# A decoder layer on one core: the score matmuls of query and key in scaled fp16 halves instead of fp32r and fp32

## The chip, the cores and the metric

The kernel runs on one core of one Trainium2 chip, in one launch. The metric is the device time of the launch in microseconds (us). The core has TensorE (PE; its weight loads are shown apart as PEld), VectorE (DVE), ScalarE (ACT), GpSimd (POOL) and SyncE (SP), which here only issues transfers. Engines run their own instruction streams and meet at semaphores.

## The reference

A decoder layer for 8 batches of 256 tokens, 512 wide. The change is in its first part, a linear attention with decay over 16 heads of 128:

```python
qkv = jax.nn.silu(x @ Wqkv.T).reshape(b, n, h, 3 * d)      # b, n, h, d = 8, 256, 16, 128
q, k, v = jnp.split(qkv, 3, axis=-1)
# in blocks of 64 with a carried state; written out, for i >= j:
#   out[i] = sum_j  exp(-s * (i - j)) * (q[i] . k[j]) * v[j]
rms = jax.lax.rsqrt(jnp.mean(out * out, axis=-1, keepdims=True) + eps)
gate = jax.nn.sigmoid(x @ Wg.T)
x = layernorm(x + (gate * (out * rms * norm_w)) @ Wo.T)
x = layernorm(x + wkv(time_decay, time_first, x, ctx))     # a recurrence over the 256 tokens
x = layernorm(x + bitlinear(gelu(bitlinear(x, w_fc)), w_proj))   # ternary weights, 512 -> 2048 -> 512
```

All inputs and the output are fp32.

## The kernel before

The attention is worked head by head: 8 *pairs* of heads, 8 *units* in a pair. Unit t of a pair is head t % 2 on token group t // 2, 512 tokens, which are two batches of 256. There are 64 units. A unit projects Q, K and G (the gate) with three fp16 matmuls for each of 4 slices of the 512 inputs (`project`; x and the weights are split in fp16 halves `x_hi`, `x_lo`, `w_hi`, `w_lo`, scaled so that they fit, and the product hi*lo + lo*hi + hi*hi is taken), ScalarE evacuates Q and K through Silu to fp32 tiles `q_t` and `k_t` with the product of the inverse scales, `dq`, as its scale, and V is projected for both heads at once (`project_v`). The halves of a head's weights are made by VectorE (`split_w`), the halves of x by ScalarE and VectorE (`split_x`), both from bounds that TensorE spreads over the partitions (`w_bound`, `x_bound`, with a matmul by ones).

For each of a unit's two batches `scores` makes keys by queries. Since a query sees only earlier keys, keys 0 to 127 meet all 256 queries (256 columns), keys 128 to 255 only the last 128 (128 columns). The wide part takes three fp32r matmuls of halves (`q_hi`, `q_lo`, `k_hi`, `k_lo`, where the k halves are made for the first keys only), the narrow part one fp32 matmul of `k_t` and `q_t`, which the trace shows as two records. VectorE multiplies both parts by the decays into `probs` (`mask`), splits them (`split_probs`), and `mix` multiplies by V. VectorE then gates the result (`gate`: `gated`, `u_hi`, `u_lo`), and `output` multiplies by Wo; VectorE adds the four token tiles of each unit to `resid` (`add_y`).

The order of every engine is written out by hand. TensorE's for unit u is: scores of unit u - 1, projection of Q, two tiles of output of unit u - 2, projection of K, two more tiles, mix of unit u - 1, projection of G, projection of V. VectorE's for unit u:

```python
                    mask(u - 1, 1 - i, 0)
                    mask(u - 1, 1 - i, 1)
                    split_v(u - 1, (t - 1) % PER_PAIR)
...
                    split_probs(u - 1)
                split_q(u)
...
                split_k(u)
...
                if not (t == 7 or last_pair and t == 7):
                    dequant(p, t + 1)
```

with the adds between these, and behind `dequant` (which makes `dq` for the next unit) the splits of weights (t = 0, 7), a chunk of the feed-forward weights (after_unit) and the gate. Pair 0 also splits x for the other groups; the last pair also starts the recurrence of the second part (`input_sum`, `bb_states`, `aa_states`, `correct`, and on GpSimd `weighted`, `numerator` and others), so that the third part can follow at once. Between pair 2 and pair 3 all engines pass through the mean of the feed-forward weights (`abs_two`).

Of the kernel before, what the change touches and what calls it, by code (L numbers as in the profile page):

```python
# [41 lines left out]
def decoder_layer(nc, x_t, x_rows, ctx_t, w_heads, slopes, norm_w, decay, first, w_ffn, out):  # L42
# [6 lines left out]
    with ExitStack() as ctx:  # L49
# [45 lines left out]
        dqv = sb("dqv", [P, GROUPS])  # L95
        stats = sb("stats", [P, 4, BT, 6])
# [40 lines left out]
        q_hi = sb("q_hi", [P, GT], F32R, att)  # L137
        q_lo = sb("q_lo", [P, GT], F32R, att)
        k_hi = sb("k_hi", [P, 2, P], F32R, att)
        k_lo = sb("k_lo", [P, 2, P], F32R, att)  # L140
# [62 lines left out]
        wmax_ok, wbound_ok, winv_ok = sem("wmax_ok"), sem("wbound_ok"), sem("winv_ok")  # L203
        wscale_ok, whalf_ok, dq_ok = sem("wscale_ok"), sem("whalf_ok"), sem("dq_ok")
# [178 lines left out]
        def _(pe):  # L383
# [48 lines left out]
            def scores(u, b):  # L432

                pe.wait_ge(q_split, u + 1)
                pe.wait_ge(k_split, u + 1)
                wait(pe, masked, 2 * u + b - 1)
                o = b * SEQ
                wide = SC[b][:, 0:SEQ]
                mm(wide, k_hi[:, b, :], q_hi[:, o:o + SEQ], start=True, stop=False)
                mm(wide, k_hi[:, b, :], q_lo[:, o:o + SEQ], start=False, stop=False)  # L440
                mm(wide, k_lo[:, b, :], q_hi[:, o:o + SEQ], start=False, stop=True)
                mm(SC[b][:, SEQ:SEQ + P], k_t[:, o + P:o + SEQ], q_t[:, o + P:o + SEQ],  # L442
                   start=True, stop=True).then_inc(scored, 1)
# [267 lines left out]
        def _(act):  # L711
# [100 lines left out]
            def unit(p, t, first_pair=False, last_pair=False):  # L812
# [5 lines left out]
                split_q(u)  # L818
# [6 lines left out]
                split_k(u)  # L825
# [162 lines left out]
        def _(dve):  # L988
# [59 lines left out]

            def dequant_v(g):
# [713 lines left out]
```

## Time and profile before

| | |
|---|---|
| time, median of 3 runs | 1334.83 us (1333.92 to 1334.94) |
| profiled execution, its own time | 1334.65 us |
| its span | 1332.9 us |
| granted TensorE clock, mean | 0.995 |
| attention (pairs 0 to 7) | from the start to about 1050 us |
| TensorE, VectorE, ScalarE, GpSimd busy | 97%, 73%, 47%, 22% |

The profile is one execution. Its own time and its span differ by 1.75 us around the first and last instruction. Busy time counts the length of instructions; a matmul's record is longer than the time after which the next one can start, since they overlap, so what a matmul costs is read from the distance of starts in the timeline and not from its length.

### The profile page before, as it was taken

To read this page: it belongs to the slowest core of one execution; us is meant where nothing else is said; L and a number is where in the kernel's file an instruction comes from. 1 tells how busy PE (TensorE), PEld (TensorE's weight loads), DVE (VectorE), ACT (ScalarE), POOL (GpSimd) and SP (SyncE) were. 2 spreads that over 40 slices of the span, in tenths; PEclk is the share of its full clock that TensorE was granted. 3 is DMA by queue.
4 is the path that set the end of the run, shared out by engine and by line. 5 is a ranking of instruction groups with operands and counts; after the bars stand their busy time and mean duration, and the time that the engine had idled before them with its cause. 6 is when DMAs were issued, how large, how long until landed. Compare 5 with 4: busy or idle time off the path is not lost.

```text
span 1332.9 us, 20153 instructions
## 1 busy us (share of the span) xinstructions
PE 1289.5 (97%) x7468; PEld 830.8 (62%) x7468; DVE 967.8 (73%) x1882; ACT 629.6 (47%) x1138; POOL 298.2 (22%) x213
## 2 busy tenths in 40 slices
PE   5899999999999999999999999999998999999997
PEld 3566666666666666666666666666665555555553
DVE  6875776696577667766776677667678788998763
ACT  3443343344333433533353344334356678888854
POOL 2112111111110111111111111111125565555630
PEclk9999999999999999999999999999999999999999
DMA  5100021121111111011111110001010111110000
GB/s 186 60 17 16 25 88 32 48 80 64 33 65 32 48 32 41 24 49 32 40 53 36 32 49 32 32 16 41 1 48 17 33 32 48 48 48 32 17 17 32
DMA packets 19103, 55.83 MB, mean 42 GB/s; under 512 B 2624, under 2 KB 2624, under 8 KB 18624
## 3 DMA queue, kind: packets, MB, share of 16 engines
q1 hardware_dynamic: 19008, 54.55, 12.3%
q8 instruction: 61, 1.00, 0.3%
q14 instruction: 34, 0.28, 0.1%
HBM read 50.35 MB, written 4.19 MB: 41 GB/s over the span
## 4 chain that ended last, share of the span: by engine, by line
PE 59%; DVE 5%; ACT 3%; issue 2%; POOL 1%; ACTq 0%; POOLq 0%; DVEq 0%
PE bank L399 7%; PE bank L400 7%; PE bank L401 7%; PE bank L613 4%; PE bank L614 4%; PE bank L471 3%; PE bank L473 3%; PE bank L472 3%; PE bank L414 3%; PE bank L416 2%; PE bank L415 2%; PE bank L639 2%; PE bank L638 2%; PE bank L459 1%; PE bank L442 1%
## 5 line engine op out<-in xcount | busy, mean ns | idle before, releaser
L399 PE MATMUL bank<-x_hi,w_hi 128*128 128x512 f16 x768 | 294.6, 384 | 5.2 <-DVE w_lo L1076 2.9
L1122 DVE TENSOR_TENSOR resid<-resid,bank 128x512 f32<-128x512 f32 x256 | 173.2, 686 | 173.5 <-PE bank L473 172.9
L400 PE MATMUL bank<-x_lo,w_hi 128*128 128x512 f16 x768 | 293.8, 383 | 0.0
L401 PE MATMUL bank<-x_hi,w_lo 128*128 128x512 f16 x768 | 293.2, 382 | 0.0
L1578 POOL TENSOR_TENSOR sq_sum<-sq_sum,o_sq 128x512 f32<-128x512 f32 x64 | 106.6, 1665 | 797.0 <-ACT o_sq L757 797.0
L757 ACT ACTIVATE o_sq<-bank 128x512 f32<-128x512 f32 x64 | 38.3, 599 | 287.9 <-DVE gated L1128 287.9
L414 PE MATMUL bank<-wv_hi,x_hi 128*128 128x256 f16 x512 | 139.6, 273 | 1.0 <-DVE x_lo L1137 0.6
L416 PE MATMUL bank<-wv_hi,x_lo 128*128 128x256 f16 x512 | 139.6, 273 | 0.0
L415 PE MATMUL bank<-wv_lo,x_hi 128*128 128x256 f16 x512 | 139.6, 273 | 0.0
L399 PEld LDWEIGHTS bank<-x_hi,w_hi 128*128 128x128 f16 x768 | 76.5, 100 | 91.9 <-issue 19.9
L401 PEld LDWEIGHTS bank<-x_hi,w_lo 128*128 128x128 f16 x768 | 75.7, 99 | 92.5 <-issue 3.3
L471 PE MATMUL bank<-wo_hi,u_hi 128*128 128x512 f32 x256 | 122.8, 480 | 3.2 <-DVE resid L1122 2.8
L400 PEld LDWEIGHTS bank<-x_lo,w_hi 128*128 128x128 f16 x768 | 75.7, 99 | 70.6 <-issue 2.2
L1094 DVE TENSOR_TENSOR probs<-bank,decays 128x256 f32<-128x256 f32 x128 | 53.9, 421 | 88.8 <-PE bank L442 52.9
L744 ACT ACTIVATE q_t<-bank,dq 128x512 f32<-128x512 f32 x64 | 44.1, 689 | 125.6 <-PE bank L401 125.4
L744 ACT ACTIVATE k_t<-bank,dq 128x512 f32<-128x512 f32 x64 | 44.0, 688 | 121.4 <-PE bank L401 121.4
L473 PE MATMUL bank<-wo_hi,u_lo 128*128 128x512 f32 x256 | 101.2, 395 | 0.0
L613 PE MATMUL bank<-tern,xq_hi 128*128 128x512 f16 x256 | 97.1, 379 | 3.0 <-ACT hid L883 3.0
L472 PE MATMUL bank<-wo_lo,u_hi 128*128 128x512 f32 x256 | 99.7, 390 | 0.0
L614 PE MATMUL bank<-tern,xq_lo 128*128 128x512 f16 x256 | 97.0, 379 | 0.0
L638 PE MATMUL bank<-tern,hq_hi 128*128 128x512 f16 x256 | 97.0, 379 | 0.0
L639 PE MATMUL bank<-tern,hq_lo 128*128 128x512 f16 x256 | 97.0, 379 | 0.0
(174 smaller groups left out, 2660.2 us busy)
## 6 DMA issues: line engine op xcount, KB each, us to landing
w_raw<-w_ffn SPq DMA_DIRECT2D x32, 512.0 KB, 3.5
raw_a<-w_heads SPq DMA_DIRECT2D x32, 256.0 KB, 3.8
raw<-w_heads SPq DMA_DIRECT2D x15, 512.0 KB, 3.6
raw<-w_heads SPq DMA_DIRECT2D x18, 256.0 KB, 3.9
x_in<-x_rows SPq DMA_DIRECT2D x8, 512.0 KB, 3.8
out<-y_out SPq DMA_DIRECT2D x8, 512.0 KB, 2.6
resid<-x_t SPq DMA_DIRECT2D x3, 1024.0 KB, 8.0
val<-ctx_t SPq DMA_DIRECT2D x6, 512.0 KB, 3.5
```

Of the source, the lines that this page charges most:

```text
L399: mm(bk[:, :], a, c, start=kt == 0, stop=False)
L400: mm(bk[:, :], a, d, start=False, stop=False)
L401: last = mm(bk[:, :], b, c, start=False, stop=kt == KT - 1)
L414: mm(to[:, o:o + 2 * DH], a, e, start=kt == 0, stop=False)
L415: mm(to[:, o:o + 2 * DH], a, f, start=False, stop=False)
L416: last = mm(to[:, o:o + 2 * DH], b, e, start=False, stop=kt == KT - 1)
L471: mm(YB[tt % 2][:, :], u_hi[:, c], wo_hi[:, i, :], start=True, stop=False)
L472: mm(YB[tt % 2][:, :], u_hi[:, c], wo_lo[:, i, :], start=False, stop=False)
L473: mm(YB[tt % 2][:, :], u_lo[:, c], wo_hi[:, i, :], start=False, stop=True).then_inc(y_done, 1)
L613: mm(FC[f % 2][:, :], xq_hi[:, t, kt, :], w, start=kt == 0, stop=False)
L614: last = mm(FC[f % 2][:, :], xq_lo[:, t, kt, :], w, start=False, stop=kt == KT - 1)
L1122: tt(resid[:, 4 * g + t, :], resid[:, 4 * g + t, :], YB[t % 2][:, :], ALU.add).then_inc(y_added, 1)
```

## The change

The four tiles of halves become fp16 and cover all 512 keys and queries. Before they are rounded, q and k are multiplied by a scale each, `qk_scale`, which VectorE works out for each unit from `dq` (`score_scales`: three small instructions in a chain, behind each `dequant`); the product of the inverse scales, `s_dq`, goes into the masks, which become scalar_tensor_tensor instructions with that scalar read from memory. ScalarE's rounding of q and k takes the scale, and VectorE's low halves too. Both parts of the scores now take three fp16 matmuls. A spare tile keeps the other tiles where they were. Its core:

```diff
-        q_hi = sb("q_hi", [P, GT], F32R, att)
-        q_lo = sb("q_lo", [P, GT], F32R, att)
-        k_hi = sb("k_hi", [P, 2, P], F32R, att)
-        k_lo = sb("k_lo", [P, 2, P], F32R, att)
+        q_hi = sb("q_hi", [P, GT], F16, att)
+        q_lo = sb("q_lo", [P, GT], F16, att)
+        k_hi = sb("k_hi", [P, GT], F16, att)
+        k_lo = sb("k_lo", [P, GT], F16, att)
+        sb("spare1", [P, GT], F32, att)
...
-                wide = SC[b][:, 0:SEQ]
-                mm(wide, k_hi[:, b, :], q_hi[:, o:o + SEQ], start=True, stop=False)
-                mm(wide, k_hi[:, b, :], q_lo[:, o:o + SEQ], start=False, stop=False)
-                mm(wide, k_lo[:, b, :], q_hi[:, o:o + SEQ], start=False, stop=True)
-                mm(SC[b][:, SEQ:SEQ + P], k_t[:, o + P:o + SEQ], q_t[:, o + P:o + SEQ],
-                   start=True, stop=True).then_inc(scored, 1)
+                for out, k0, q0, q1 in ((SC[b][:, 0:SEQ], o, o, o + SEQ), (SC[b][:, SEQ:SEQ + P], o + P, o + P, o + SEQ)):
+                    kh, kl = k_hi[:, k0:k0 + P], k_lo[:, k0:k0 + P]
+                    mm(out, kh, q_hi[:, q0:q1], start=True, stop=False)
+                    mm(out, kh, q_lo[:, q0:q1], start=False, stop=False)
+                    last = mm(out, kl, q_hi[:, q0:q1], start=False, stop=True)
+                last.then_inc(scored, 1)
...
-            def split_q(u):
+            def split_q(u, t):
                 act.wait_ge(evacuated, PROJ * u + Q + 1)
-                fn(q_hi[:, :], q_t[:, :], ACT.Copy).then_inc(q_hi_ok, 1)
-
-            def split_k(u):
+                act.wait_ge(qk_scale_ok, u + 1)
+                fn(q_hi[:, :], q_t[:, :], ACT.Identity, scale=qk_scale[:, t % 2, t // 2, 0:1]).then_inc(q_hi_ok, 1)
+
+            def split_k(u, t):
                 act.wait_ge(evacuated, PROJ * u + K + 1)
-                fn(k_hi[:, :, :], first_keys(k_t), ACT.Copy).then_inc(k_hi_ok, 1)
+                fn(k_hi[:, :], k_t[:, :], ACT.Identity, scale=qk_scale[:, t % 2, t // 2, 1:2]).then_inc(k_hi_ok, 1)
...
+            def score_scales(p, t):
+
+                u, g, i = PER_PAIR * p + t, t // 2, t % 2
+                dve.wait_ge(dq_ok, u + 2)
+                ts(qk_inv[:, i, g, :], dq[:, i, g, 0:2], 131072.0, TINY, ALU.mult, ALU.add).then_inc(qk_inv_ok, 1)
+                dve.wait_ge(qk_inv_ok, u + 1)
+                v.reciprocal(qk_scale[:, i, g, :], qk_inv[:, i, g, :]).then_inc(qk_scale_ok, 1)
+                ts(s_dq[:, i, g:g + 1], qk_inv[:, i, g, 0:1], qk_inv[:, i, g, 1:2], None, ALU.mult).then_inc(s_dq_ok, 1)
...
-                tt(probs[:, b, 0:SEQ], SC[b][:, 0:SEQ], decays[:, i, :], ALU.mult).then_inc(masked_off, 1)
-                tt(probs[:, b, SEQ:SEQ + P], SC[b][:, SEQ:SEQ + P], decays[:, i, 0:P], ALU.mult).then_inc(masked, 1)
-
-            def split_q(u):
+                stt(probs[:, b, 0:SEQ], SC[b][:, 0:SEQ], c, decays[:, i, :], ALU.mult, ALU.mult).then_inc(masked_off, 1)
+                stt(probs[:, b, SEQ:SEQ + P], SC[b][:, SEQ:SEQ + P], c, decays[:, i, 0:P], ALU.mult,
+                    ALU.mult).then_inc(masked, 1)
+
+            def split_q(u, t):
                 dve.wait_ge(q_hi_ok, u + 1)
                 wait(dve, scored, 2 * u)
-                tt(q_lo[:, :], q_t[:, :], q_hi[:, :].bitcast(F32), ALU.subtract).then_inc(q_split, 1)
-
-            def split_k(u):
+                stt(q_lo[:, :], q_t[:, :], qk_scale[:, t % 2, t // 2, 0:1], q_hi[:, :], ALU.mult,
+                    ALU.subtract).then_inc(q_split, 1)
+
+            def split_k(u, t):
                 dve.wait_ge(k_hi_ok, u + 1)
-                tt(k_lo[:, :, :], first_keys(k_t), k_hi[:, :, :].bitcast(F32), ALU.subtract).then_inc(k_split, 1)
+                stt(k_lo[:, :], k_t[:, :], qk_scale[:, t % 2, t // 2, 1:2], k_hi[:, :], ALU.mult,
+                    ALU.subtract).then_inc(k_split, 1)
...
                 if not (t == 7 or last_pair and t == 7):
                     dequant(p, t + 1)
+                    score_scales(p, t + 1)
...
                     dequant(p + 1, 0)
+                    score_scales(p + 1, 0)
...
             dequant(0, 0, K, V)
+            score_scales(0, 0)
             split_w(0, 0, K, 2)
```

TensorE, the scores of unit 0, between the projection of V (`wv_hi`, `x_lo`) and the next projection of Q (`x_hi`, `w_hi`), before:

```order
L416 MATMUL bank<-wv_hi,x_lo 128x256
L430 MATMUL bank<-wmax,ones 128x3
L439 MATMUL bank<-q_hi,k_hi 128x256
L440 MATMUL bank<-q_lo,k_hi 128x256
L441 MATMUL bank<-q_hi,k_lo 128x256
L442 MATMUL bank<-q_t,k_t 128x128
L439 MATMUL bank<-q_hi,k_hi 128x256
L440 MATMUL bank<-q_lo,k_hi 128x256
L441 MATMUL bank<-q_hi,k_lo 128x256
L442 MATMUL bank<-q_t,k_t 128x128
L399 MATMUL bank<-x_hi,w_hi 128x512
```

and now (the first batch, and the start of the second, which is the same):

```order
L421 MATMUL bank<-wv_hi,x_lo 128x256
L435 MATMUL bank<-wmax,ones 128x3
L445 MATMUL bank<-q_hi,k_hi 128x256
L446 MATMUL bank<-q_lo,k_hi 128x256
L447 MATMUL bank<-q_hi,k_lo 128x256
L445 MATMUL bank<-q_hi,k_hi 128x128
L446 MATMUL bank<-q_lo,k_hi 128x128
L447 MATMUL bank<-q_hi,k_lo 128x128
L445 MATMUL bank<-q_hi,k_hi 128x256
```

In place of one fp32 matmul of 128 columns stand three fp16 ones; nothing else of TensorE has moved.

VectorE in unit 0, from the low halves of q and k to the split of unit 1's weights (`w_hi`, `w_lo`), before:

```order
L1100 TENSOR_TENSOR q_lo<-q_t,q_hi 128x512
L1104 TENSOR_TENSOR k_lo<-k_t,k_hi 128x256
L1013 TENSOR_REDUCE wmax<-raw 128x3
L1025 TENSOR_SCALAR winv<-bank 128x3
L1027 RECIPROCAL wscale<-winv 128x3
L1030 TENSOR_SCALAR winv<-winv 128x1
L1047 TENSOR_SCALAR dq<-winv,xinv 128x3
L1073 TENSOR_SCALAR w_hi<-raw,wscale 128x512
L1076 SCALAR_TENSOR_TENSOR w_lo<-raw,wscale,w_hi 128x512
```

and now:

```order
L1118 SCALAR_TENSOR_TENSOR q_lo<-q_t,qk_scale,q_hi 128x512
L1123 SCALAR_TENSOR_TENSOR k_lo<-k_t,qk_scale,k_hi 128x512
L1019 TENSOR_REDUCE wmax<-raw 128x3
L1031 TENSOR_SCALAR winv<-bank 128x3
L1033 RECIPROCAL wscale<-winv 128x3
L1036 TENSOR_SCALAR winv<-winv 128x1
L1053 TENSOR_SCALAR dq<-winv,xinv 128x3
L1059 TENSOR_SCALAR qk_inv<-dq 128x2
L1061 RECIPROCAL qk_scale<-qk_inv 128x2
L1062 TENSOR_SCALAR s_dq<-qk_inv 128x1
L1088 TENSOR_SCALAR w_hi<-raw,wscale 128x512
L1091 SCALAR_TENSOR_TENSOR w_lo<-raw,wscale,w_hi 128x512
```

The three scale instructions stand between `dq` and the weights' split, and k_lo is twice as wide.

## Rows read from the trace of the kernel before

**Rows 1.** The page's busy time, share and instructions of each engine.

```profile
PE 1289.5 (97%) x7468; PEld 830.8 (62%) x7468; DVE 967.8 (73%) x1882; ACT 629.6 (47%) x1138; POOL 298.2 (22%) x213
```

**Rows 2.** Windows: stretch, length, busy us of each engine, clock, DMA share, GB/s.

```profile
145.00:270.00 125.00, 125.00 (x750) 84.49 (x748) 88.32 (x177) 47.82 (x86) 14.51 (x10) 1.00 0.16 51
...
905.00:1060.00 155.00, 145.30 (x844) 96.27 (x843) 120.80 (x230) 79.79 (x139) 51.32 (x35) 1.00 0.08 25
```

**Rows 3.** Timeline of TensorE: start us, length us, line, tiles, shape, how many.

```profile
601.13 0.27 PE L414 MATMUL bank<-wv_hi,x_hi 128*128 128x256 f16 x1
...
603.65 0.27 PE L416 MATMUL bank<-wv_hi,x_lo 128*128 128x256 f16 x1
...
603.88 0.28 PE L440 MATMUL bank<-q_lo,k_hi 128*128 128x256 f32 x1
...
604.12 0.38 PE L442 MATMUL bank<-q_t,k_t 128*128 128x128 f32 x2
...
604.70 0.38 PE L442 MATMUL bank<-q_t,k_t 128*128 128x128 f32 x2
604.91 0.38 PE L399 MATMUL bank<-x_hi,w_hi 128*128 128x512 f16 x1
...
607.29 0.38 PE L401 MATMUL bank<-x_hi,w_lo 128*128 128x512 f16 x1
```

**Rows 4.** Groups of weight loads by shape: count, busy us, mean ns.

```profile
L414 PEld LDWEIGHTS bank<-wv_hi,x_hi 128*128 128x128 f16 x512 | 50.0, 98 | 14.8 <-issue 2.4 <-DVE wv_lo L1065 0.4
...
L442 PEld LDWEIGHTS bank<-q_t,k_t 128*128 128x128 f32 x256 | 39.4, 189 | 0.0
```

**Rows 5.** Groups of VectorE by shape.

```profile
L1402 DVE SCALAR_TENSOR_TENSOR hq_lo<-bank,h_scale,hq_hi 128x512 f16<-128x512 f32 x64 | 46.8, 743 | 33.8 <-ACT hq_hi L927 33.8
L1100 DVE TENSOR_TENSOR q_lo<-q_t,q_hi 128x512 fp32r<-128x512 f32 x64 | 44.9, 701 | 0.0
L1128 DVE SCALAR_TENSOR_TENSOR gated<-g_t,bank 128x512 f32<-128x512 f32 x64 | 43.5, 679 | 1.5 <-PE bank L459 1.5
...
L1104 DVE TENSOR_TENSOR k_lo<-k_t,k_hi 128x256 fp32r<-128x256 f32 x64 | 28.0, 437 | 2.2 <-ACT k_hi L765 2.2
```

**Rows 6.** Timeline of VectorE, small instructions ahead of unit 1's weight split.

```profile
31.93 0.15 DVE L1030 TENSOR_SCALAR winv<-winv 128x1 f32<-128x1 f32 x1
32.12 0.23 DVE L1047 TENSOR_SCALAR dq<-winv,xinv 128x3 f32<-128x3 f32 x1
32.26 0.48 DVE L1073 TENSOR_SCALAR w_hi<-raw,wscale 128x512 f16<-128x512 f32 x1
```

**Rows 7.** Groups of ScalarE by shape.

```profile
L765 ACT ACTIVATE k_hi<-k_t 128x256 fp32r<-128x256 f32 x64 | 26.7, 418 | 2.0
...
L723 ACT ACTIVATE x_hi<-resid,xscale 128x512 f16<-128x512 f32 x16 | 10.2, 711 | 11.4 <-DVE xscale L1005 11.4
```

**Rows 8.** Timeline of TensorE, its waits: [us idle before <-who ended it].

```profile
18.82 0.60 PE L399 MATMUL bank<-x_hi,w_hi 128*128 128x512 f16 x1 [2.08 <-DVE w_lo L1076]
...
33.58 0.39 PE L399 MATMUL bank<-x_hi,w_hi 128*128 128x512 f16 x1 [0.82 <-DVE w_lo L1076]
...
39.29 0.50 PE L423 MATMUL bank<-xmax,ones 128*128 128x4 f32 x2 [2.94 <-DVE probs L1095]
...
66.28 0.27 PE L414 MATMUL bank<-wv_hi,x_hi 128*128 128x256 f16 x1 [0.28 <-DVE x_lo L1137]
...
398.71 0.38 PE L689 MATMUL bank<-abs_two,ones 128*128 128x2 f32 x2 [2.08 <-DVE abs_two L1276]
...
995.47 0.27 PE L414 MATMUL bank<-wv_hi,x_hi 128*128 128x256 f16 x1 [0.43 <-DVE rms_in L1498]
...
1019.29 1.09 PE L587 MATMUL bank<-ident,num 128*128 128x128 f32 x8 [1.46 <-DVE probs L1095]
...
1041.05 0.50 PE L471 MATMUL bank<-wo_hi,u_hi 128*128 128x512 f32 x1 [2.83 <-DVE resid L1122]
```

**Rows 9.** Timeline of VectorE in the last pair.

```profile
996.49 2.82 DVE L1133 TENSOR_TENSOR u_lo<-gated,u_hi 128x512 fp32r<-128x512 f32 x1
```

More of the change, by code:

```diff
@@ L95, in decoder_layer @@
         dqv = sb("dqv", [P, GROUPS])
+        qk_inv = sb("qk_inv", [P, 2, GROUPS, 2])
+        qk_scale = sb("qk_scale", [P, 2, GROUPS, 2])
+        s_dq = sb("s_dq", [P, 2, GROUPS])
         stats = sb("stats", [P, 4, BT, 6])
@@ L203, in decoder_layer @@
         wmax_ok, wbound_ok, winv_ok = sem("wmax_ok"), sem("wbound_ok"), sem("winv_ok")
+        qk_inv_ok, qk_scale_ok, s_dq_ok = sem("qk_inv_ok"), sem("qk_scale_ok"), sem("s_dq_ok")
         wscale_ok, whalf_ok, dq_ok = sem("wscale_ok"), sem("whalf_ok"), sem("dq_ok")
@@ L817, in unit @@
                 evacuate(u, t, Q, first_unit)
-                split_q(u)
+                split_q(u, t)
                 if lag1:
@@ L824, in unit @@
                 evacuate(u, t, K, first_unit)
-                split_k(u)
+                split_k(u, t)
                 if last_pair and t in (4, 5):
@@ L1088, in split_wo, with mask @@
                 tt(wo_lo[:, i, :], raw_a[:, i, :], wo_hi[:, i, :].bitcast(F32), ALU.subtract).then_inc(wo_split, 1)
-            def mask(u, i, b):
+            def mask(u, t, b):
+                i, c = t % 2, s_dq[:, t % 2, t // 2:t // 2 + 1]
                 dve.wait_ge(scored, 2 * u + b + 1)
+                dve.wait_ge(s_dq_ok, u + 1)
                 wait(dve, mixed, u)
-                tt(probs[:, b, 0:SEQ], SC[b][:, 0:SEQ], decays[:, i, :], ALU.mult).then_inc(masked_off, 1)
-                tt(probs[:, b, SEQ:SEQ + P], SC[b][:, SEQ:SEQ + P], decays[:, i, 0:P], ALU.mult).then_inc(masked, 1)
-            def split_q(u):
+                stt(probs[:, b, 0:SEQ], SC[b][:, 0:SEQ], c, decays[:, i, :], ALU.mult, ALU.mult).then_inc(masked_off, 1)
+                stt(probs[:, b, SEQ:SEQ + P], SC[b][:, SEQ:SEQ + P], c, decays[:, i, 0:P], ALU.mult,
+                    ALU.mult).then_inc(masked, 1)
+            def split_q(u, t):
                 dve.wait_ge(q_hi_ok, u + 1)
                 wait(dve, scored, 2 * u)
-                tt(q_lo[:, :], q_t[:, :], q_hi[:, :].bitcast(F32), ALU.subtract).then_inc(q_split, 1)
-            def split_k(u):
+                stt(q_lo[:, :], q_t[:, :], qk_scale[:, t % 2, t // 2, 0:1], q_hi[:, :], ALU.mult,
+                    ALU.subtract).then_inc(q_split, 1)
+            def split_k(u, t):
                 dve.wait_ge(k_hi_ok, u + 1)
-                tt(k_lo[:, :, :], first_keys(k_t), k_hi[:, :, :].bitcast(F32), ALU.subtract).then_inc(k_split, 1)
+                stt(k_lo[:, :], k_t[:, :], qk_scale[:, t % 2, t // 2, 1:2], k_hi[:, :], ALU.mult,
+                    ALU.subtract).then_inc(k_split, 1)
             def split_v(u, t):
@@ L1148, in unit @@
                         dve.wait_ge(decays_ok, 2 * p + t)
-                    mask(u - 1, 1 - i, 0)
-                    mask(u - 1, 1 - i, 1)
+                    mask(u - 1, (t - 1) % PER_PAIR, 0)
+                    mask(u - 1, (t - 1) % PER_PAIR, 1)
                     split_v(u - 1, (t - 1) % PER_PAIR)
@@ L1158, in unit @@
                     split_probs(u - 1)
-                split_q(u)
+                split_q(u, t)
                 if t == 0 and not first_pair:
@@ L1178, in unit @@
                     add_y(u - 2, gb, 3)
-                split_k(u)
+                split_k(u, t)
                 if first_pair and t in (1, 2, 4):
@@ L1510, in _ @@
             U = UNITS
-            mask(U - 1, 1, 0)
-            mask(U - 1, 1, 1)
+            mask(U - 1, PER_PAIR - 1, 0)
+            mask(U - 1, PER_PAIR - 1, 1)
             split_v(U - 1, PER_PAIR - 1)
```

## The prediction

> **What bounds the kernel now.** I read the busy line first: TensorE is busy 97% of the span, VectorE 73% [rows 1]. The windows then say where TensorE is not full. From 145 to 270 us it is busy for the whole stretch, with VectorE at 71% (88.32 of 125.00), while from 905 to 1060 us it lacks 9.7 us and VectorE is busy for 120.80 of 155.00 [rows 2]. So in the middle of the attention (pairs 1 to 6) the end moves by what a unit costs on TensorE, and VectorE's extra work is free there; at the start, at the step before pair 3 and in the last pair TensorE waits for VectorE, and there VectorE's extra work counts. The list of TensorE's waits names these places [rows 8].
>
> **TensorE, removed and added.** The two score blocks of one unit stand in the timeline [rows 3]. The 24 fp16 matmuls of 256 columns of the V projection start from 601.13 to 603.65, 0.110 us apart, so the first score matmul's turn comes at 603.76, and the next projection starts at 604.91: 1.15 us for both blocks. Inside, an fp32r matmul of 256 columns takes 0.12 (from the second at 603.88 to the fourth instruction at 604.12 is 0.24), three of them 0.36; the second block's fp32 one of 128 columns, which shows as two records, takes 0.21 (604.70 to 604.91). 2 x (0.36 + 0.215) = 1.15.
>
> After, each block has three fp16 matmuls of 256 columns and three of 128. The first three have V's shape, 0.1096 each: 0.66 for six. fp16 with 128 columns is not in the trace. From below, 128 columns can't take less than their share of the pace of wider ones: the 12 of 512 columns of a projection start from 604.91 to 607.29, 0.216 apart, 256 take 0.110, so the slope is 0.415 ns a column and 128 come to 0.056. From above, each matmul has a weight load of its own, whose record in fp16 is 98 ns long [rows 4]; if nothing of it overlapped with a matmul as short as this, the pace would be 0.098. I take 0.058, near the lower end, because loads overlap in the rows: an fp32 load's record is 189 ns long and yet its matmuls follow each other at 0.11 to 0.12, some 0.07 less, and the same 0.07 off 98 ns leaves 0.03, well below 0.056. A unit then costs 0.658 + 6 x 0.058 = 1.006 and saves 0.144 us; with 0.056 it saves 0.154, with 0.098 it loses 0.096.
>
> The Trainium skill (TensorE: Matmul & The Clock Gate, section "Back-to-back issue gap") speaks against the change. It gives about 81 ns per matmul at 128 columns for streams of loads and matmuls in real kernels, and an isolated gap of N/2.4 + 2.5 ns, which is 56 ns. By 81 ns a unit would save 0.01 us. The same sentence gives 131 ns at 512 columns, where this trace shows 215, and the isolated form gives 216; so I hold to the second.
>
> 64 units have scores. About 60 keep the saving; in the others TensorE comes to a wait on VectorE that has no TensorE work ahead of it in its chain (33.58, 39.29 and some in the last pair). 60 x 0.144 = **8.6 us gained**.
>
> **VectorE and ScalarE, added in each unit.** A scalar read from memory costs a scalar_tensor_tensor 0.063 us: 743 ns with one against 679 without, same columns, both with a PSUM operand [rows 5]. The masks are now such instructions, four a unit: +0.25. q_lo goes from 701 to about 750: +0.05. k_lo has all 512 columns: from 437 to about 750, +0.31. The three small scale instructions stand in a chain; in the rows a dependent small one starts 0.19 after the one it waits for, 0.04 after its end, and an instruction that waits for nothing new 0.14 after dq, whose scalar is in memory and which lasts 0.23 [rows 6]. dq's successor used to start 0.14 behind it; now it stands behind qk_inv (0.23 + 0.04 after dq), the reciprocal (0.19 on), s_dq (estimated half of that, 0.09, since it waits for nothing new) and s_dq's own 0.13: 0.68 against 0.14, **+0.53**. Together 1.1 us a unit. A unit lasts 15.7 us (64 of them between the waits at 33.58 and 1041.05 [rows 8]) and VectorE is idle for 29% of it in the middle, 4.6 us. On ScalarE k_hi grows from 418 to what the fp16 scaled copy of 512 columns takes, 711, +0.29 [rows 7]; q_hi gains 0.08. Both are hidden where TensorE is full: k_hi and k_lo are needed only after the projections of G and V, 12 x 0.216 + 24 x 0.11 = 5.2 us of TensorE work.
>
> **Where it is not hidden** [rows 8]. (a) Start: the scale chain stands ahead of the first split of K, whose w_lo TensorE waits for, and again ahead of unit 1's split of Q: these are the waits at 18.82 and 33.58, 0.53 each. (b) The x bound at 39.29 waits for the masks behind them, +0.25 more. (c) Two projections of V wait for the last x_lo of a group (one at 66.28, one like it at the next group); k_hi and k_lo stand ahead of it: +0.65 each, 1.3. Start together: 2.6. (d) The wait for abs_two at 398.71: k_lo and the scale chain stand ahead, +0.8. (e) Last pair: rms_in, waited for at 995.47, stands behind k_lo and the scale chain, +0.8; the masks ahead of the turn at 1019.29 stand behind k_lo, the chain and their own growth, +1.1; the add waited for at 1041.05 stands behind k_lo, the bb scans and four masks, +0.6. Together 2.5. **Sum lost: 2.6 + 0.8 + 2.5 = 5.9 us.**
>
> **The sum.** -8.6 + 5.9 = -2.7 us on the profiled execution's 1334.65, which is 0.18 below the median of the runs, 1334.83. I forecast 1332.0 us.
>
> **GpSimd in the way.** In the last pair a VectorE instruction between two SBUF tensors can stand still while GpSimd works: u_lo took 2.82 us there [rows 9], where q_lo, of the same form, has a mean of 0.70 [rows 5]. The new qk_inv, reciprocal and s_dq read SBUF alone, and everything in VectorE's queue there is shifted by about 1 us against GpSimd. An unlucky meeting costs up to one such stall, 2.1 us, and a lucky one gives as much back; this goes into the range, not the sum. The Trainium skill (SBUF — State Buffer, section "SBUF: two separate sides") calls it an exclusive lock held for the whole instruction; the row agrees.
>
> **Rivals.**
> 1. *The same mechanism, losses smaller or gains whole* (each wait takes only part of what I put on it, because its chain is anchored in TensorE work that comes earlier now): losses of 4, gain 9.2 (0.056): 1329.4. For it: several of the chains in the last pair start from an output matmul's end. With my own forecast this is the forecast's family: chance 0.50, its own range 1328.5 to 1334.
> 2. *VectorE eats it.* The gain on TensorE is real but the three places bound by VectorE cost 5.9 and one or two GpSimd stalls more, 9 in all: 1334.65 - 8.6 + 9 = 1335.0, no change: chance 0.24. It shows as TensorE's idle time at the start and from 905 to 1060 us grown by more than 8 us together.
> 3. *The weight load sets the pace at 128 columns* (the other side). Each of the six short matmuls then takes between 0.075 and 0.098. A unit saves nothing from 0.082 on (0.658 + 6 x 0.082 = 1.15), and with the losses the kernel gains nothing from 0.066 on (60 x 0.098 = 5.9). At 0.086: 1.174 a unit, +1.4 + 5.9: 1342.0. At 0.098: +5.8 + 5.9: 1346.3. Against it: 0.03 of net load time as worked out above; for it: no fp16 matmul under 256 columns in the trace, and twelve weight loads a unit where there were eight matmul instructions. Chance 0.20. The 81 ns of the Trainium skill's page above is this rival's number from outside; the sum would be 1340.2 by it.
> 4. *The change does nothing on TensorE*, since both blocks keep the same column count in passes: 3 x 256 + 4 x 128 before against 3 x 256 + 3 x 128 now. That leaves the gain of one short pass in four, 0.215 - 3 x 0.058 = 0.04 a block, and the fp32r surcharge of 0.01 on each of six matmuls; these two are the 0.144. If a change of type between neighbouring matmuls costs what they bring, the losses alone remain: 1334.65 + 5.9 = 1340.6. A chance of 0.06 is left for it; the rows show no such cost (from V's fp16 through fp32r and fp32 back to fp16 the durations add up with nothing over).
>
> **How the numbers follow.** 0.2% (2.7 us) is about what a measurement of this kernel tells from no change. The forecast's family lies on both sides of -2.7: 0.36 of its 0.50 beyond it, with some of rival 2 (0.04) faster, 0.40. Rival 2 mostly, the rest of the forecast and the mild end of rival 3 are within 0.2%: 0.35. Most of rival 3, rival 4 and the bad end of rival 2 are slower: 0.25. The range goes from 1328.5 (gain 9.2, losses 3) to 1340 (rival 3 at 0.080): 0.8 of the time.
>
> **What would show it.** In the profile after: two score blocks between the last V matmul and the next projection in 1.00 us instead of 1.15, 128-column fp16 matmuls starting 0.056 to 0.060 apart; masks 60 ns longer; k_lo of about 750; TensorE fully busy from 145 to 270 us; the waits of L399 at 18.82 and 33.58 grown from 2.08 and 0.82 to 2.6 and 1.4 us, the one for abs_two from 2.08 to 2.9. It is wrong if the short matmuls stand 0.08 or more apart, if TensorE begins to wait for p_lo or u_lo in the middle pairs, or if the last pair's waits grow by more than 5 us.

## The result, and the profile after

The changed kernel takes 1338.9 us (median of 7 runs, 1337.42 to 1339.73), the kernel before 1334.25 in the runs beside it (median of 7): a ratio of 1.0030, with a 95% interval from 1.0019 to 1.0042. It is slower, by 2.5 to 5.6 us, where 2.7 faster was forecast. The profiled execution took 1339.13 us with a span of 1337.4.

The page's first line, after, which answers to [rows 1]:

```profile
PE 1285.9 (96%) x7596; PEld 817.0 (61%) x7596; DVE 1033.0 (77%) x2074; ACT 652.3 (49%) x1138; POOL 298.0 (22%) x213
```

TensorE works less than before, VectorE 65.2 us more, which is 1.02 us for each of 64 units. The timeline of TensorE at the two score blocks, which answers to [rows 3]:

```profile
605.72 0.27 PE L445 MATMUL bank<-q_hi,k_hi 128*128 128x256 f16 x1
...
606.04 0.22 PE L445 MATMUL bank<-q_hi,k_hi 128*128 128x128 f16 x1
606.10 0.22 PE L446 MATMUL bank<-q_lo,k_hi 128*128 128x128 f16 x1
606.16 0.22 PE L447 MATMUL bank<-q_hi,k_lo 128*128 128x128 f16 x1
606.21 0.27 PE L445 MATMUL bank<-q_hi,k_hi 128*128 128x256 f16 x1
...
606.71 0.38 PE L404 MATMUL bank<-x_hi,w_hi 128*128 128x512 f16 x1
```

Both blocks take 0.99 us, and the 128-column matmuls start 0.056 us apart. So the gain is there, and the loss must lie in waits. The windows that answer to [rows 2]:

```profile
145.00:270.00 125.00, 124.53 (x768) 83.04 (x767) 96.63 (x202) 50.63 (x87) 14.83 (x10) 1.00 0.16 51
...
905.00:1060.00 155.00, 144.45 (x834) 92.99 (x833) 127.18 (x247) 80.75 (x134) 48.68 (x33) 0.97 0.08 25
```

Two things differ from what was foreseen: TensorE is idle for 0.47 us in the stretch from 145 to 270, which was to stay full, and its clock is 0.97 in the last pair, where it was 1.00. How the two traces drift apart is best read where each unit's projection of Q starts (its first matmul of x_hi and w_hi, in the two timelines, in us; the differences are those of the unrounded starts):

| unit | before | after | after less before |
|---|---|---|---|
| 1 | 33.58 | 35.68 | +2.10 |
| 5 | 101.70 | 105.32 | +3.62 |
| 14 | 241.91 | 244.83 | +2.92 |
| 15 | 257.39 | 260.79 | +3.39 |
| 23 | 381.89 | 384.76 | +2.87 |
| 25 | 418.45 | 421.69 | +3.24 |
| 59 | 947.43 | 947.35 | -0.08 |
| 63 | 1015.08 | 1019.10 | +4.01 |
| end of the span | 1332.9 | 1337.4 | +4.5 |

In a middle unit the changed kernel gets 0.16 to 0.19 us ahead, 0.17 on average, so 64 units bring 10.9 us. Once in every pair, from unit 14 to 15 for instance, it falls back by 0.47 instead. It is level just ahead of the last pair's fourth unit, and loses 4 us in four units there. The waits of TensorE, in groups, show the new one of the middle (engine, its line, whose line it waited for: us in total, times, longest):

```profile
PE bank L404 <- DVE w_lo L1091: 4.2, 2, 2.6
...
PE bank L419 <- DVE wv_lo L1080: 3.3, 7, 0.5
...
PE bank L694 <- DVE abs_two L1299: 2.9, 1, 2.9
PE bank L461 <- DVE p_lo L1135: 2.7, 2, 1.7
...
PE bank L419 <- DVE x_lo L1157: 1.9, 2, 1.0
PE bank L419 <- DVE rms_in L1521: 1.6, 2, 1.2
```

**The wait that I missed.** In the seventh unit of a pair VectorE makes the next pair's V weights, behind k_lo and the scale chain in its order; TensorE's projection of V, in that same unit, needs them. The timeline of all engines, before:

```profile
126.18 0.42 DVE L1104 TENSOR_TENSOR k_lo<-k_t,k_hi 128x256 fp32r<-128x256 f32 x1
126.52 0.22 DVE L1047 TENSOR_SCALAR dq<-winv,xinv 128x3 f32<-128x3 f32 x1
...
127.56 1.28 DVE L1065 SCALAR_TENSOR_TENSOR wv_lo<-raw_a,wvscale,wv_hi 128x1024 f16<-128x1024 f32 x1
...
129.12 0.27 PE L414 MATMUL bank<-wv_hi,x_hi 128*128 128x256 f16 x1
```

And the same place after:

```profile
129.61 0.75 DVE L1123 SCALAR_TENSOR_TENSOR k_lo<-k_t,qk_scale,k_hi 128x512 f16<-128x512 f32 x1
...
130.28 0.22 DVE L1053 TENSOR_SCALAR dq<-winv,xinv 128x3 f32<-128x3 f32 x1
...
130.53 0.17 DVE L1059 TENSOR_SCALAR qk_inv<-dq 128x2 f32<-128x2 f32 x1
130.74 0.17 DVE L1061 RECIPROCAL qk_scale<-qk_inv 128x2 f32<-128x2 f32 x1
130.82 0.19 DVE L1062 TENSOR_SCALAR s_dq<-qk_inv 128x1 f32<-128x1 f32 x1
...
130.93 0.22 DVE L1076 TENSOR_SCALAR dqv<-xinv,wvinv 128x4 f32<-128x4 f32 x1
...
131.84 1.29 DVE L1080 SCALAR_TENSOR_TENSOR wv_lo<-raw_a,wvscale,wv_hi 128x1024 f16<-128x1024 f32 x1
...
133.18 0.28 PE L419 MATMUL bank<-wv_hi,x_hi 128*128 128x256 f16 x1 [0.47 <-DVE wv_lo L1080]
```

Before, wv_lo ended at 128.84 and TensorE came to it at 129.12: 0.28 us of slack, and no row of a wait. From the start of k_lo to the start of wv_lo there were 1.38 us, now there are 2.23: 0.85 more, which eats the slack and leaves a wait. A wait reads too short in such a row, since a matmul's record (0.38 long) reaches beyond the next one's turn (0.216): the step from 0.17 ahead to 0.47 behind says 0.64 us, seven times, 4.5 us.

**The clock.** Windows of 5 us in the last pair, after (busy us of each engine, and in the third column from the end the granted clock):

```profile
1010.00:1015.00 5.00, 3.32 (x13) 1.96 (x12) 5.00 (x5) 3.62 (x9) 4.50 (x3) 0.61 0.00 0
1015.00:1020.00 5.00, 5.00 (x26) 2.41 (x24) 4.79 (x10) 2.15 (x4) 3.36 (x3) 0.70 0.02 3
...
1045.00:1050.00 5.00, 5.00 (x17) 1.95 (x16) 4.61 (x11) 0.92 (x1) 0.13 (x1) 0.66 0.14 54
```

Before, the clock is 1.00 in these windows. After, TensorE runs at 1.2 GHz from 1011.1 to 1018.0 and from 1045.3 to 1048.7: at two waits for p_lo (0.97 and 1.68 us; the clock falls within the second) and behind one for the sum of the residual (2.99). The timeline shows it as matmuls of 512 columns 0.43 us apart instead of 0.216. The two kernels have the other half-clock stretches in common: one at some 20, one at 40 and one at 402 us, 3.4 us each, all behind waits of 2.1 to 3.2 us.

### The profile page after: what moved, and what is told of

Its sections match the earlier page's. It is cut to its first block, busy times and chain, and to the rows that moved or that the text cites. A ratio compares the mean times of both kernels' runs of the same rounds, so it can differ in the third digit from the quotient of the medians.

```text
span 1337.4 us, 20686 instructions
## 1 busy us (share of the span) xinstructions
PE 1285.9 (96%) x7596; PEld 817.0 (61%) x7596; DVE 1033.0 (77%) x2074; ACT 652.3 (49%) x1138; POOL 298.0 (22%) x213
## 3 DMA queue, kind: packets, MB, share of 16 engines
q8 instruction: 62, 1.02, 0.3%
## 4 chain that ended last, share of the span: by engine, by line
PE 82%; DVE 10%; issue 4%; ACT 3%; POOL 1%; DMA 0%; SPq 0%; ACTq 0%; POOLq 0%; DVEq 0%
PE bank L404 11%; PE bank L405 11%; PE bank L406 11%; PE bank L419 4%; PE bank L476 4%; PE bank L421 4%; PE bank L420 4%; PE bank L478 4%; PE bank L477 4%; PE bank L618 4%; PE bank L619 4%; PE bank L643 2%; PE bank L644 2%; PE bank L464 2%; PE bank L445 2%
## 5 line engine op out<-in xcount | busy, mean ns | idle before, releaser
L1111 DVE SCALAR_TENSOR_TENSOR probs<-bank,s_dq,decays 128x256 f32<-128x256 f32 x128 | 61.1, 478 | 58.3 <-PE bank L447 29.7
```

## The experiments

All were timed in 5 rounds beside the kernel before, whose median was 1334.97, 1335.08 and 1335.11 us in the three sets. My theory: the loss is waits made by VectorE's queue order, above all the V weights. The rivals: TensorE's clock; the masks and the fp16 scores themselves.

**1. V weights early** (e2_wv_early). In the unit function of VectorE:

```diff
+                if t == 6 and not last_pair:
+                    split_v_weights(p + 1)
                 split_k(u, t)
...
-                if t == 6 and not last_pair:
-                    split_v_weights(p + 1)
```

> The changed kernel with one thing moved: in the seventh unit of a pair VectorE makes the next pair's wv_lo ahead of k_lo and the scale chain, as it has room for it, and not behind them. My theory (queue order: wv_lo stands behind 0.31 of k_lo and 0.52 of scale chain, its slack was 0.28, and each of seven first V matmuls comes 0.64 us late) expects the wait of L419 at 133.18 and its six fellows to be gone and the time 7 x 0.64 = 4.5 us below the changed kernel: 1334.4, with the last pair's waits and its half-clock stretches unchanged. Rival 1 (the wait only moves: k_lo or the split of the next unit's Q weights, both now 1.3 us later, becomes the next wait) expects a new wait in TensorE's row of 0.3 us or more in the same units and 1337.5 to 1339. Rival 2 (the loss lies in TensorE's clock, half for 6.8 and 3.4 us in the last pair, not in queue order) expects the seven waits to be gone, but the time to follow the clock: 1334.4 only if the two stretches stay, 1331 if a changed phase removes them.

Measured: 1335.3 us (11 runs, 1333.45 to 1336.21), ratio to before 1.0002 (0.9993 to 1.0011), 3.6 below the changed kernel. No wait for wv_lo is left in TensorE's row, k_lo comes 2.1 us later in its unit and nobody waits for it, and the step at unit 15 is 0.16 ahead as in any other. This wait was most of the slowdown. That only 3.6 of the 4.5 us show has two reasons. The kernel before was itself slower in this set: against it the changed kernel stood at +4.65 us and this one stands at +0.33, which is 4.3 less. And the last pair's half clock did not stay as it was. The seven steps of the trace return 4.5 us in full; 1.3 us are lost ahead of the first projection (it starts at 13.60 instead of 12.30), 1.25 behind abs_two, where the half clock lasts 6.8 us instead of 3.4, and 1.7 come back in the last pair, where it lasts 3.4 us (from 1009.5) instead of 10.2.

**2. The chain late** (e1_chain_late). score_scales behind the gate, at the start behind the splits of K and G:

```diff
                 if not (t == 7 or last_pair and t == 7):
                     dequant(p, t + 1)
-                    score_scales(p, t + 1)
...
                 if lag1:
                     gate(u - 1)
+                if not (t == 7 or last_pair and t == 7):
+                    score_scales(p, t + 1)
...
```

> The changed kernel with the scale chain (qk_inv, reciprocal, s_dq) moved to the end of VectorE's unit, so that it stands behind wv_lo, w_lo and u_lo, and, at the start, behind the split of K and G. By queue order 0.52 of 0.83 us ahead of wv_lo is gone, which leaves 0.64 - 0.52 = 0.12 of each of the seven V waits (-3.6 us), 0.5 at each of the two first waits (-1.0), 0.5 at abs_two and some 0.5 to 1 in the last pair: about 1333. The rival for the start (the wait at 18.82 grew because TensorE's clock rose at another moment, not because the chain stands ahead) expects that wait to stay at 2.6. If q_hi, which needs qk_scale on ScalarE, becomes late for the scores, a new wait of L399 on q_lo shows in every unit and the time is 1340 or more.

Measured: 1339.64 us (1338.15 to 1341.72), ratio 1.0037, where some 1333 was expected. What was expected of the moved waits came true: the first wait for w_lo is 2.08 again and the second 1.08 (2.60 and 1.60 in the changed kernel), and the steps of the V waits fell from 0.47 to -0.05, which leaves the 0.12 lost. But the chain met something else in its new place. The group of qk_inv in this kernel (busy us, mean ns):

```profile
L1059 DVE TENSOR_SCALAR qk_inv<-dq 128x2 f32<-128x2 f32 x64 | 80.0, 1250 | 0.0
```

It took 169 ns in the changed kernel. Its timeline with GpSimd's shows why:

```profile
53.31 1.61 POOL L1603 TENSOR_TENSOR sq_sum<-sq_sum,o_sq 128x512 f32<-128x512 f32 x1 [37.54 <-ACT o_sq L762]
53.70 2.98 DVE L1059 TENSOR_SCALAR qk_inv<-dq 128x2 f32<-128x2 f32 x1
...
54.86 1.80 POOL L1597 MEMSET resid<- 128x2048 f32 x1
```

Two elements a partition took 2.98 us, until GpSimd's two instructions were through, and the mean of 1250 ns says that it was held up in most units. The x bound stands behind them: 2.88 us of wait where there was 0.19; the wait for abs_two is 3.89. So a chain of small instructions is not cheap everywhere, and "behind the gate" is the worst of the two places tried. The Trainium skill (SBUF — State Buffer, section "SBUF: two separate sides") has an exclusive lock between the two engines for some VectorE instructions; qk_inv behaves as if it were one of them.

**3. No scales** (e3_no_scale). The halves are those of the unscaled query and key (ACT.Copy, plain subtraction), the mask a plain product, and score_scales is gone:

```diff
-                stt(probs[:, b, 0:SEQ], SC[b][:, 0:SEQ], c, decays[:, i, :], ALU.mult, ALU.mult).then_inc(masked_off, 1)
+                tt(probs[:, b, 0:SEQ], SC[b][:, 0:SEQ], decays[:, i, :], ALU.mult).then_inc(masked_off, 1)
```

> The changed kernel without the scales: the fp16 halves are those of the unscaled query and key, the masks are plain products of scores and decays, and nothing of qk_inv, qk_scale and s_dq is left. TensorE's part (six fp16 matmuls a block) is whole, and so is k_lo with all 512 columns. By my theory VectorE has 0.25 (masks), 0.05 (q_lo) and 0.52 (chain) less a unit; k_lo's 0.31 stays and stands ahead of wv_lo, 0.03 more than the slack of 0.28, so the seven waits go to about 0.1 each. With the whole gain of TensorE (60 x 0.16 = 9.6) and losses of 0.7 there, 0.6 at the start, 0.3 at abs_two and 1.0 in the last pair: 1334.25 - 9.6 + 2.6 = 1327.3. The rival (what is lost lies in TensorE's clock or in the fp16 scores themselves) expects 1332 or more, with half-clock stretches in the last pair as in the changed kernel.

Measured: 1329.04 us (1327.34 to 1329.57), ratio 0.9954 (0.9941 to 0.9966), 1.7 us above what was expected and 3 below the rival. That is 9.9 below the changed kernel with the same matmuls: the fp16 scores bring what they should, and the scales take it all back and 4 us more. The half-clock stretches are there as well (at 1003.5 and 1034.2, 3.4 us each), 3.4 us less of them than in the changed kernel, so the clock can be only a small part of what sets these two apart; unit by unit the traces differ by 4.05 us at the seven V weights, 2.9 at the start and 2.5 in the last pair.

**4. The chain alone in the kernel before** (e4_chain_alone): score_scales with its three tiles added at the same places, its results unused.

> The kernel before with the scale chain alone added in VectorE's order, its results unused; scores, masks and halves are those of before. TensorE gains nothing. By queue order: 0.52 at each of the two first waits (+1.0), 0.52 less the slack of 0.28 at each of the seven V waits (+0.24 each, 1.7), 0.5 at abs_two, 1.0 in the last pair: +4.2, 1338.5. The prediction on record (nothing lost in the middle) would have +2.5: 1336.8. A rival that puts the loss on the masks and k_lo expects less than +1.5.

Measured: 1344.03 us (1341.84 to 1344.6), ratio 1.0064 (1.005 to 1.0077): +9, twice what was expected. The queue-order part is as worked out: +0.53 at the second w_lo wait (1.35), 0.32 at each of the seven V projections (this kernel's at 132.16 starts 3.04 later than before, the unit ahead of it 2.73), 0.53 at abs_two (2.61), 0.52 at rms_in. The rest, some 5 us, isn't queue order, and nearly all of it falls in three places with half clock: from 40.0 to 46.9, from 1016.3 to 1019.7 and from 1047.0 to 1053.8, where the kernel before has 3.4 us at the first and nothing at the two others (the steps there are +1.36, +1.40 and +2.05 us). GpSimd did not hold the chain up: the longest of its 64 qk_inv took 171 ns.

**5. Plain masks alone** (e6_masks_plain): the changed kernel with the product above and everything else, the chain too, as it was; the scale stays in the probabilities.

> The changed kernel with masks that are plain products of scores and decays, 0.06 us shorter each; the scale is not divided out of the probabilities; the scale chain and the scaled halves stay. Theory (only the places that TensorE waits for count, and the chain is most of the loss): masks are 0.25 a unit and stand ahead of the x bound, of wv_lo in the seven units, of rms_in and of the last pair's turn: 0.2 x 7 off the V waits if all of that unit's queue shifts, or nothing if that queue's start is anchored in ScalarE's k_hi; with the start and the last pair 0.5 to 2.5 us below the changed kernel, 1336.5 to 1338.4. The rival (masks cost as much as the chain, and the 9.9 us between the changed kernel and the one without scales is theirs) expects 1334 or less.

Measured: median 1340.01 us, but in two groups: eight of the 11 runs between 1339.3 and 1340.7 with a mean granted clock of 0.988 to 0.990, three at 1335.6, 1336.3 and 1337.9 with 0.992 and 0.993. Between 1336.5 and 1338.4 was expected, and the median missed it. The seven V waits are 0.46 to 0.47 as in the changed kernel: the masks have no part in them. They count at the x bound (2.95 instead of 3.19) and in units 11 and 19, where the loss of 0.2 us each is gone (-0.18, a step as any other). The trace is of the fastest run (1335.62), so it doesn't say what the median's runs did. What the groups show is that executions of one and the same kernel with a lower mean clock are some 3 to 4 us longer.

**6. Filling the waits of the last pair.** Matmuls that feed nothing, into a bank whose next projection starts afresh:

```diff
+            def fill(bk, n, g=0):
+                for _ in range(n):
+                    mm(bk[:, :], x_hi[g][:, 0, 0:P], x_hi[g][:, 0, :], start=True, stop=True)
...
                 for b in range(2):
+                    fill(PJ[(PROJ * (t + 1) + G) % 2], fills[b], GROUPS - 1)
                     pe.wait_ge(masked, 2 * u + b + 1)
```

> The changed kernel with ten matmuls that feed nothing (fp16, 512 columns, into a bank whose next projection starts afresh), 3 in TensorE's wait for p_lo at 1008.45 and 7 in the one at 1010.24 of the last pair, so that these two waits of 0.97 and 1.68 are all but filled. Theory (part of the loss is TensorE's clock: it falls to 1.2 GHz behind these waits, from 1011.1 to 1018.0 in the profiled run): the half-clock stretch behind them goes, 16 matmuls of the G projection run 0.216 apart instead of 0.43, 3.4 us less TensorE work, of which the wait at the turn (1.35 in the run with early V weights, 0 in the changed kernel) takes 1.4 to 1.5 back: 1 to 2 us below the changed kernel, 1337 to 1338. Rival (the clock there follows something else, or nothing waits for those matmuls): the stretch stays, or goes without a change of time, 1338.9.

Measured: 1339.53 us (1338.84 to 1340.2). I had them in the eighth unit's mix; the two waits are in the seventh's and stayed 0.97 and 1.68. It doesn't test the theory, and the 2.2 us of extra TensorE work there cost nothing that is clear of noise (ratio 1.0033, where the changed kernel's interval is 1.0019 to 1.0042). The next run has them in their place (e9_fill_mix, `t == 6`).

> The changed kernel with the ten empty matmuls where they were meant to go: 3 and 7 in the two waits for p_lo of the last pair's seventh unit (0.97 and 1.68 in the profile). The run before had them one unit later, where they stood ahead of no such wait. Theory (the half clock from 1011.1 to 1018.0 comes from these waits): the idle time before the two p_hi matmuls reads 0.3 and 0.2 instead of 0.97 and 1.68, no half clock from 1011 to 1018, the next projection's matmuls 0.216 apart, TensorE 3.4 us ahead there, of which the wait at the turn (none in the changed kernel, 1.35 with the shorter half-clock stretch) takes 3 back, since the masks ahead of it are VectorE's: 0.3 to 1.5 us less, 1337.4 to 1338.6. If the next turn's wait takes all of it: 1338.9. The rival (clock independent of waits) expects the half-clock stretch within 3 us of where it was.

Measured: 1340.72 us (1340.13 to 1342.23), ratio 1.0041 (1.0029 to 1.0054), above the 1337.4 to 1338.6 that was expected. Windows of this kernel:

```profile
1010.00:1015.00 5.00, 4.52 (x26) 2.43 (x24) 5.00 (x5) 4.64 (x10) 4.33 (x3) 1.00 0.00 0
1015.00:1020.00 5.00, 4.91 (x31) 2.60 (x30) 4.83 (x12) 0.82 (x3) 2.94 (x3) 1.00 0.02 3
1020.00:1025.00 5.00, 2.54 (x13) 1.87 (x12) 3.42 (x7) 4.15 (x7) 2.94 (x2) 0.86 0.00 0
```

The half clock behind the two waits is gone, as the clock theory had it, and the time is not lower: TensorE now waits 2.46 us for the masks at the turn (1020.72 to 1023.18), and the clock falls behind that wait instead. Filling one hole moved the loss to the next, since there the last pair waits for VectorE anyway. What the stretch at 1011 cost by itself this run can't say, as a new one came behind the next wait.

**7. No scales, better order** (e7_no_scale_early): run 3 with wv_lo ahead of k_lo, and k_lo behind the last two x_lo of the first pair's groups and, in the sixth unit of the last pair, behind rms_in (and the chunk of weights that after_unit makes).

> The kernel without scales (1329.0) with the next pair's wv_lo ahead of k_lo, and with k_lo behind the last two x_lo of a group in the first pair and behind rms_in in the sixth unit of the last pair. By queue order: 7 x 0.06 at the V waits, 0.45 at each of two x_lo waits (0.75 before, 0.28 then), 0.7 at the rms_in wait: 2.0 us less, 1327.0. Rival: the unscaled kernel's time is set elsewhere at these places (gate, masks), less than 0.7 gained, 1328.4 or more.

Measured: 1326.59 us (1325.71 to 1327.35), ratio 0.9936. The waits for x_lo and rms_in are gone from TensorE's row.

**8. That, with filled waits.** 7 empty matmuls ahead of the second projection, 11 ahead of the second x bound, 9 ahead of abs_two (e8_fills, still with the misplaced ten).

> The kernel just described with matmuls that feed nothing in four of TensorE's waits: 7 ahead of the second projection (wait 2.08), 11 ahead of the second x bound (2.95), 9 ahead of abs_two (2.37), and the ten of the last pair. If the half-clock stretches (from 20.5, 41.0, 399.4 and 1003.5 for 3.4 us each in the run without scales) come from these waits, they go, and each gives back up to 1.7 us of TensorE work where TensorE sets the pace behind it: 1.7 at 41, 1.7 at 399, and 0.5 to 1.5 at the two others, whose gain a wait on VectorE takes: 4 to 6 us less, 1321 to 1323. Rival (the clock follows the clock's own schedule, or the waits grow by as much as the work shrinks): 1327.

Measured: 1321.97 us (1320.36 to 1322.71), ratio 0.9898 (0.9883 to 0.9914). Then with twelve (5 and 7) in the two waits of the last pair's seventh unit instead of the ten, 6 at the turn and 11 in the wait for the residual (e10_no_scale_fills):

> The kernel without scales, with wv_lo and rms_in early and with empty matmuls in its waits, now with the last pair's where the waits are (5 and 7 in the seventh unit), 6 at the turn wait of the eighth (1.69) and 11 in the wait for the sum of the residual (2.84), behind which the clock was half from 1028.4 to 1031.8. Theory: the last half-clock stretch goes, 1.7 us of fc matmuls come earlier, and the misplaced ten (2.2 us of TensorE work on the path, partly in later waits) cost no more: 1.5 to 3 us below 1322.0, 1319 to 1320.5. The rival (those matmuls were free and the stretch cost nothing) expects 1322.

Measured: 1320.06 us (1319.46 to 1320.94), ratio 0.9886 (0.9872 to 0.9899), the fastest of all. The windows of the run without fills (run 7), then of this one, show what the empty matmuls do:

```profile
36.00:46.00 10.00, 7.05 (x31) 3.57 (x30) 8.72 (x18) 5.99 (x10) 0.00 (x0) 0.83 0.35 124
395.00:410.00 15.00, 14.13 (x73) 8.87 (x74) 10.10 (x28) 4.03 (x8) 1.07 (x1) 0.89 0.14 53
990.00:1010.00 20.00, 16.85 (x75) 9.29 (x74) 19.29 (x25) 13.76 (x22) 15.32 (x9) 0.83 0.09 27
```

```profile
36.00:46.00 10.00, 9.43 (x58) 5.58 (x56) 8.87 (x22) 4.96 (x9) 0.00 (x0) 1.00 0.22 81
395.00:410.00 15.00, 15.00 (x95) 10.15 (x94) 12.64 (x22) 6.21 (x11) 1.67 (x1) 1.00 0.00 1
990.00:1010.00 20.00, 19.00 (x101) 10.67 (x100) 18.28 (x28) 11.31 (x21) 10.43 (x7) 1.00 0.01 1
```

**9. The same repair for both kernels.** Fills in the kernel before (e12_before_fills), and in the changed kernel, scales and all, with early V weights (e11_scaled_fills), so that two kernels with nearly nothing but full clock stand against each other. The numbers of empty matmuls are fitted to each one's waits (7, 11, 8 before and 9, 12, 11 now at the start and at abs_two; 3 and 7, 6, 11 in both in the last pair).

> The kernel before with empty matmuls in the same waits (7, 11, 8, 3 and 7, 6, 11), the measure against which the repaired versions stand. Its profiled run has half clock at 18.9, 39.4 and 401.2 for 3.4 us each and none in the last pair; by the clock theory each gives back up to 1.7, the first less: 4 us, 1331. Rival (the clock counts only with the change): 1335.

> The changed kernel, scales and all, with both repairs: the next pair's wv_lo ahead of k_lo (1335.3 alone) and empty matmuls in its waits (9, 12, 11 at the start and abs_two, 3 and 7, 6, 11 in the last pair). Theory (VectorE's queue order and TensorE's clock are the whole of what ate the gain): three half-clock stretches at the start and at abs_two and one or two in the last pair go, 5 us as in the kernel without scales: 1330. Rival (the scale chain costs more than these two): 1333 or more.

Measured: before with fills 1331.31 us (1330.25 to 1331.97), ratio 0.9971; changed with both repairs 1329.2 us (1328.23 to 1329.83), ratio 0.9953. Their mean clock is 0.998 in all runs but one, 0.999. At full clock the change with early V weights is worth 2.1 us, and the same scores without scales and in the better order 11.25.

## Why the prediction was wrong

**Right: what TensorE saves, and what VectorE's instructions cost.** Pace 0.056 (0.058 taken), two blocks 0.99 (1.006), masks 478 and 341 ns, 60 more than before, k_lo 763 (750), the chain 0.65 from dq to what follows it (0.68). The saving was too low: 0.17 a unit instead of 0.144, and taken for all 64 units (also those that wait later, whose waits are then counted against it) it is 10.9 us, not 8.6. The weight-load rival and the type-change rival fell with these rows, and with them the 81 ns of the Trainium skill (TensorE: Matmul & The Clock Gate, section "Back-to-back issue gap"), whose isolated 56 ns is what the trace shows.

**The step that failed** is "in the middle of the attention (pairs 1 to 6) ... VectorE's extra work is free there". I read TensorE as full from 145 to 270 and VectorE as idle for 29%, and I named one consumer only: "k_hi and k_lo are needed only after the projections of G and V". The rule that I should have kept is the other one, what is queued behind a grown instruction. Behind k_lo stands wv_lo, and it had 0.28 us of slack, which a list of waits can't show, since a slack leaves no row. Cost: 4.5 us in the trace, 3.6 to 4.3 in the time by run 1. The prediction's sign of being wrong looked at p_lo and u_lo in the middle pairs, and nothing waited for these. The same step failed in one smaller place: in units 10 and 18 the masks start late, behind GpSimd's new decays, and their growth of 0.25 us stands ahead of the sum that frees a bank for TensorE's next output tile:

```profile
187.42 0.48 DVE L1111 SCALAR_TENSOR_TENSOR probs<-bank,s_dq,decays 128x256 f32<-128x256 f32 x1 [3.23 <-POOL decays L1591]
...
189.06 1.28 DVE L1142 TENSOR_TENSOR resid<-resid,bank 128x512 f32<-128x512 f32 x2
...
189.80 0.19 PEld L476 LDWEIGHTS bank<-wo_hi,u_hi 128*128 128x128 f32 x1 [0.44 <-DVE resid L1142]
```

That is 0.2 us for each of the two, in the steps at units 11 and 19, and with plain masks (run 5) it is gone.

**The step that was not in the sum: TensorE's clock.** The kernel before gains 3.8 us from fills (1335.11 to 1331.31), the changed kernel with early V weights 6.1 (1335.3 to 1329.2), 2.3 us more by medians. The profiled pairs put only part of this down to the clock: 1.2 us at abs_two, behind which the half clock lasts 6.8 us in run 1 and 3.4 in the kernel before; 1.5 lie ahead of the first projection (13.60 and 12.08 us), where no empty matmul stands, 0.7 go the other way at the start, and the last pair gives nothing. In the changed kernel itself the clock's place is the last pair. Read from the unit table, with 0.17 added for each unit's saving, it loses 5.4 us there with 10.2 us of half clock; run 1 loses 3.8 with 3.4 us, and the two runs of part 9 differ there by 3.8 with none. So 1.7 us is what its half clock cost, and the shorter stretch cost nothing that shows.

**Mis-sized: the losses where VectorE is waited for.** The two runs of part 9, both at full clock, read unit by unit as in the table and with 0.17 added for each unit's saving, show 4.9 us at the start (2.6 predicted), 0.75 at abs_two (0.8) and 3.75 in the last pair (2.5). At the start (a) is 0.52 at the first wait, as said, but 0.78 at the second (0.53 for the chain, by run 4, and 0.27 that run 3 has without any scale), and (c) is 0.7 each, but there are three V projections that wait for x_lo, not two: the one that the half clock at 40 hid, 0.75 already in the kernel before with fills and 1.45 now. The x bound of the next group lost 0.4 more. One more us there is not the change's order at all: TensorE's clock rose at 15.0 us in the one and at 17.0 in the other. In the last pair a wait for rms_in came up at the fourth unit too (0.37).

**The account**, in us between the two profiled executions, unit by unit as in the table: -10.9 saved, +4.5 at the start (units 1 to 6), +4.5 at the V weights, +0.4 in units 11 and 19, +0.7 at abs_two, +5.4 in the last pair (3.75 at full clock and 1.7 of half clock): +4.6, against +4.5 between their spans and +4.65 between the medians (1338.9 less 1334.25). Forecast was -8.6 + 2.6 + 0.8 + 2.5. That the 1338.9 lies inside the stated range is luck: the range reached up there for the sake of rival 3, whose slow matmuls did not come. Rival 2 (VectorE eats it, chance 0.24) was nearest in kind, but it had no change of time; it named the three known places and GpSimd stalls, and not the middle. Its sign did not come either: from 0 to 66 us TensorE is idle for 18.74 us where it was 17.06, from 905 to 1060 for 10.55 where it was 9.70 (a matmul at half clock counts as busy, which hides a part). I found no stall of the chain by GpSimd in the changed kernel (the longest of 64 qk_inv took 172 ns); run 2 shows what one costs.

**Open.** Why only pairs 1 and 2 have the small wait for the masks (units 10 and 18); and how much of the last pair's 3.75 us is order and how much is GpSimd's, which wasn't taken apart. That the scales could be made elsewhere (once for a pair, or on another engine) wasn't tried; run 3 only shows what is to be had, for this input, without them.

## What to carry to other kernels

Before you call work free because its engine is idle a third of the time, list what is queued behind it up to the engine's next real wait, and for each such product the time between its end and its use: 0.85 us of growth against a slack of 0.28 that no list of waits shows cost 4.5 us here, as much as the whole slowdown. A small dependent chain of three instructions cost 0.5 us at each place that TensorE waited behind it, and moved next to GpSimd's work up to 3. And where an engine with a clock of its own waits 2 to 3 us, price what comes behind the wait at half clock too; empty matmuls in such waits gave 3.8 to 6.5 us here (not in every wait: run 6 gained nothing).

## What the runs showed of the hardware

- TensorE fell to 1.2 GHz for 3.4 or 6.8 us at or behind waits of 1.7 to 3.9 us (in every profiled run without fills, near 20, 40 and 400 us), and not once between 16.0 and 1313 us when these waits were nearly filled with matmuls that feed nothing (the last run of part 8).
- Which waits of the last pair were followed by half clock changed from kernel to kernel with nearly equal waits: 0.81 and 1.68 us in the kernel before, and the clock stayed whole; 0.82 and 1.69 in run 4, and it fell. Behind the wait for the sum of the residual, 2.99 us in the changed kernel and in run 1, it fell in the first and stayed whole in the second.
- The moment of the first rise lay between 15.0 and 19.6 us. In the three profiled kernels with the old scores it was 15.0, 15.5 and 16.1, in the others 16.0 to 19.6, with the same work ahead of it. I have no cause for that.
- A tensor_scalar of 128x2 elements with both ends in SBUF waited up to 2.98 us for GpSimd (run 2), where it takes 0.17 in the changed kernel.
